# A fused routed feed-forward kernel: block turns on VectorE for the routing, a fifth bank for the first tiles, and a new order of the routing steps

## The chip, the cores and the metric

The kernel runs on one core of one Trainium2 chip. The metric is the device time of one execution in microseconds (us), lower is better. The core has five engines that run their own lists of instructions side by side and meet at semaphores: TensorE (PE, with its weight loads shown as PEld), VectorE (DVE), ScalarE (ACT), GpSimd (POOL) and SyncE (SP), which here only starts transfers. TensorE writes into PSUM, eight banks of 128 partitions by 512 fp32 columns.

## The reference

`x` holds 4 batches of 1024 tokens by 512 features. Each batch has one of 64 condition matrices; eight experts follow, and each token goes to one of them, at most 512 tokens an expert.

```python
h = einsum('bsd,bdh->bsh', x, cond_W[itok]) + cond_b[itok]      # 4096 tokens
probs = softmax(h @ Wr)                      # 8 experts
eidx = argmax(probs);  p_tok = probs[eidx]
rank = number of earlier tokens with the same expert;  keep = rank < 512
xe = h[tokens of expert e, by rank]
ye = (relu(xe @ W1[e]) @ W2[e]) * p_tok      # 512 x 2048, 2048 x 512
out = x + scatter(ye)
```

## The kernel before

**Precision.** The large products are made of three passes over a high and a low part of each operand. ACT copies the high part, VectorE subtracts it to get the low one. A token tile's condition product is 4 blocks of k by 3 passes, twelve matmuls of 512 columns (L1318).

**The stages.** The 32 tiles of 128 tokens (8 chunks of 4 tiles, 2 chunks a batch) go through the condition product first. The first four run together (`first_tiles`, L1302 and L1306) and each later one by `cond_tile`. VectorE's `store_h` adds the bias and writes the tile to `rows` (L864), which frees the bank (`s_accf`). POOL stores whole chunks to memory (L496), SP the last eight tiles one by one (L432). Then the rows of expert 0 are gathered: the early tokens by four indirect transfers from memory (L532), and TensorE turns them into PSUM (L1380); the last four tiles' tokens are added by selection products (L1371). After that an expert loop of Strassen-like W1 products (L1404, L1418) and W2 products (L1506) fills the rest of the time.

**Routing, between the tiles.** The logits are not computed from `h` but from x with a small matrix M = W Wr of the batch, in plain fp32. The steps of a batch are put behind tiles by lists at L50 to L55: the entry for batch b is the tile after which the step runs.
- `M_TURN` (L1208): TensorE multiplies the transposed condition matrix by Wr, in four column groups of 32, for batch 0 with the bias products before it (L1220); ACT copies the result to `m_rows` (L640).
- `M_SUM` (L1228): TensorE turns `m_rows` into PSUM (L1231), and VectorE's `copy_m` writes it to `m32` (L854).
- `ROUTE` (L1233): TensorE multiplies x of the batch's two chunks by M (L1244), 64 products. ACT copies the logits with their bias to `logits_t` (`copy_logits`, L645).
- `CHOOSE`: TensorE turns the logits so that tokens lie on partitions (`by_token`, L1254); VectorE's `choose` takes the maximum and the one-hot rows (L874 to L893); ACT takes the exponentials (L654).
- `PLACE`: TensorE counts ranks (L1262); VectorE's `place` makes the payload and eight selection matrices (L899 to L918).
- `FILL`: TensorE adds the batch to the table of slots (L1273). After the last, the table is turned within the next tile (`turn_table`), and VectorE makes the token lists (`make_tokens`, L967).

`choose_late` (L922) runs on VectorE after the store of tile `PLACE[-1] + 2`. The splits of chunk c stand at tiles `SPLIT_X[c]` (two halves), those of batch b's condition weights at `SPLIT_W[b]` (four blocks), and the first W1 splits at `SPLIT_W1`.

**What sets the order.** Each engine takes its list as written out. For tile n ACT does, in this order, `copy_turned`, `copy_logits`, `exps`, splits of x, splits of W, table copy, W1 split (L679 to L700). VectorE does `store_h`, `choose`, `copy_m`, `place`, `choose_late`, `make_tokens`, late parts, splits of x, of W, of W1 (L1010 to L1037). TensorE does the tile, turn, by-token turn, fill, M turn, rank, route (L1345 to L1358). A low split waits for ACT's high split; `copy_m` must be done before the route; a chunk's load waits for the route that reads the buffer's old chunk.

**Banks.** Three banks serve the tiles in turn, `y_ps` bank 3 the fourth of the first four tiles. So tile 4 waits until tile 0 is stored:

```python
def cond_bank(n):
    return y_ps[:, 3, :] if n == TPC - 1 else cond_ps[n if n < TPC else (n - TPC) % 3]
...
pe.wait_ge(s_accf, n - 3 if n < TPC + 3 else n - 2)
```

**Loads.** SP issues in the order of L354 to L461: condition blocks and x chunks first, then as buffers fall free. Ahead of the first tiles TensorE runs `keep_warm(12)` on zeros (L1336).

Of the kernel before, what the change touches and what calls it, by code (L numbers as in the profile page):

```python
# [17 lines left out]
def moe_kernel(nc, x, x_t, cat, cond_w, cond_wt, cond_b, cond_br, w_r, w_1, w_2, out, h_rows):  # L18
    f32, f32r = mybir.dt.float32, mybir.dt.float32r
    bf16, f16, u32 = mybir.dt.bfloat16, mybir.dt.float16, mybir.dt.uint32  # L20
    ALU = mybir.AluOpType
# [29 lines left out]
    M_SUM = [5, 10, 13, 18]  # L51
    ROUTE = [6, 11, 15, 20]
    CHOOSE = [8, 13, 18, 23]
    PLACE = [10, 15, 20, 25]
    FILL = [13, 18, 23, 27]  # L55

    SPLIT_X = [None, None, (3, 4), (6, 7), (12, 14), (16, 17), (21, 22), (22, 24)]
    SPLIT_W = [None, (4, 4, 5, 5), (11, 11, 12, 13), (16, 17, 18, 19)]
# [4 lines left out]
    SPLIT_W1 = {NT - 9: 0, NT - 8: 3}  # L63
# [23 lines left out]
    with ctx:  # L87
# [39 lines left out]
        m_rows = sb("m_rows", [P, P], f32)  # L127
        ident = sb("ident", [P, P], f32)
# [64 lines left out]
        def cond_bank(n):  # L193
            return y_ps[:, 3, :] if n == TPC - 1 else cond_ps[n if n < TPC else (n - TPC) % 3]
# [3 lines left out]
        turned_ps = y_ps[:, 1, 0:CPB * P].rearrange("p (c n) -> p c n", c=CPB)  # L198
        tok_ps = y_ps[:, 1, 0:CPB * P].rearrange("p (t g) -> p t g", t=TPB)[:, :, 0:E]
# [3 lines left out]
        m_ps = y_ps[:, 3, 0:P]  # L203
        bias_ps = y_ps[:, 3, P:P + BATCH]
        turn_ps = y_ps[:, 3, 2 * P:3 * P]
        logits_ps = tp_ps[:, 0, 0:CPB * P]
        held = [logits_t[:, :, :].rearrange("p c n -> p (c n)"), m32[:, :, :, :].rearrange("p b k g -> p (b k g)")]
# [14 lines left out]
        s_m = sem("m_product_done")  # L222
# [8 lines left out]
        s_lg = sem("logits_done")  # L231
# [110 lines left out]
        def _(sp):  # L342
# [64 lines left out]

            load_next_xt(4)
            load_cond(2)
# [3 lines left out]
            load_next_xt(6)  # L413
            load_next_xt(7)
            load_cond(3)
            sp.wait_ge(s_turn, 3)
            load_cond_wt(3)

# [193 lines left out]
        def _(act):  # L612
# [23 lines left out]
            def copy_turned(b):  # L636
                act.wait_ge(s_turn, b + 1)
                if b >= 1:
                    act.wait_ge(s_m, b)
                nc.scalar.activation(m_rows[:, :], turn_ps, ACTF.Copy).then_inc(s_turnc, 1)  # L640

            def copy_logits(b):
                act.wait_ge(s_mcopy, b + 1)
                act.wait_ge(s_lt, CPB * (b + 1))
                nc.scalar.activation(logits_t[:, :, :].rearrange("p c n -> p (c n)"), logits_ps, ACTF.Identity,  # L645
                                     bias=bias_g[:, b:b + 1]).then_inc(s_ltc, 1)
# [176 lines left out]
        def _(dve):  # L823
# [24 lines left out]
            def copy_m(b):  # L848
                dve.wait_ge(s_m, b + 1)
                if b >= 2:  # L850
                    dve.wait_ge(s_ltc, b - 1)
                if b == 0:
                    nc.vector.tensor_copy(bias_g[:, :], bias_ps)
                nc.vector.tensor_copy(m32[:, b % 2, :, :].rearrange("p k g -> p (k g)"), m_ps).then_inc(s_mcopy, 1)  # L854
# [16 lines left out]
            def choose(b):  # L871

                dve.wait_ge(s_lg, b + 1)
                then(nc.vector.tensor_reduce(top[:, :], tok_ps, AX.X, ALU.max))  # L874
# [3 lines left out]
                nc.vector.tensor_tensor(diff[:, :, :], tok_ps, wide(top[:, :]), ALU.subtract  # L878
# [326 lines left out]
        def _(pe):  # L1205
            PARTS = ((HI, HI), (HI, LO), (LO, HI))

            def m_turn(b):  # L1208
# [13 lines left out]
                for k in range(DK):  # L1222
                    for g in range(NQ):
                        last = nc.tensor.matmul(turn_ps[g * G:(g + 1) * G, :], wr32[:, k, :],  # L1224
                                                stage[:, 0, k, g * P:(g + 1) * P], start=(k == 0), stop=(k == DK - 1))
                last.then_inc(s_turn, 1)

            def m_sum(b):  # L1228

                pe.wait_ge(s_turnc, b + 1)  # L1230
                nc.tensor.transpose(m_ps, m_rows[:, :], ident[:, :]).then_inc(s_m, 1)  # L1231

            def route(b):  # L1233
# [4 lines left out]
                for h in range(CPB):  # L1238
                    c = CPB * b + h
                    if c >= 1:  # L1240
                        pe.wait_ge(s_xin[c % 4], 16 * (c // 4 + (c % 4 > 0)))
                    for k in range(DK):
                        for g in range(NQ):
                            last = nc.tensor.matmul(logits_ps[g * G:(g + 1) * G, h * P:(h + 1) * P], m32[:, b % 2, k, :],  # L1244
                                                    x_in[c % 4][:, k, g * P:(g + 1) * P],
                                                    start=(k == 0), stop=(k == DK - 1))
                    last.then_inc(s_lt, 1)

            def by_token(b):
                pe.wait_ge(s_ltc, b + 1)  # L1250
                if b >= 1:
                    pe.wait_ge(s_oh, b)
                for c in range(CPB):
                    last = nc.tensor.transpose(turned_ps[:, c, :], logits_t[:, c, :], ident[:, :])  # L1254
                last.then_inc(s_lg, 1)
# [84 lines left out]
            keep_warm(KEEP_FIRST)  # L1340
# [4 lines left out]
            for n in range(TPC, NT):  # L1345
# [235 lines left out]
```

## Time and profile before

| | |
|---|---|
| time, median of 3 runs | 800.9 us (799.99 to 800.93) |
| profiled execution, its own time | 800.89 us |
| its span, first to last instruction | 799.0 us |
| PE busy | 791.0 us, 99% |
| DVE busy | 581.1 us, 73% |
| POOL busy | 517.1 us, 65% |
| ACT busy | 351.5 us, 44% |
| mean granted TensorE clock | 0.999 |

The profile is of one execution; its time of 800.89 us is 1.9 us over the span, which runs from the first to the last instruction. Times in the views are microseconds from the span's start. In a view by time a line gives start, length, engine, source line, operation, output and inputs and the count of merged instructions. In brackets stands how long the engine was idle before it, and what ended that. Matmuls overlap, so lengths of single ones add to more than the time they take together; the chain of work gives lengths without the overlap.

### The profile page before, as it was taken

How to read it: one execution, taken by the hardware profiler on the slowest of the kernel's cores; microseconds unless marked ns; L12 is line 12 of the kernel's file. 1: busy time of each engine (PE TensorE's matmuls, PEld its weight loads, DVE VectorE, ACT ScalarE, POOL GpSimd, SP SyncE). 2: the span in 40 equal slices, each digit the busy share in tenths (PEclk: the TensorE clock that was granted, in tenths of full speed). 3: DMA queues.
4: the chain of work that ended last, by engine and by line, in shares of the span. 5: the costliest groups of instructions: out<-in, count | busy, mean ns of one | idle time of the engine just before them, and what ended most of it. 6: DMA issues, size and time to landing. Idle time of an engine off the chain costs nothing.

```text
span 799.0 us, 14228 instructions
## 1 busy us (share of the span) xinstructions
PE 791.0 (99%) x5267; PEld 703.7 (88%) x5267; DVE 581.1 (73%) x760; ACT 351.5 (44%) x537; POOL 517.1 (65%) x392
## 2 busy tenths in 40 slices
PE   8999999999999999999999999999999999999997
PEld 5787889899999999999999999999999999999996
DVE  5677878889767896589658965797578866895532
ACT  4322336446444544445444544454445444554430
POOL 1000138898887688777887688768876888663601
PEclk9999999999999999999999999999999999999999
DMA  8987645542544255534453444435541544255201
GB/s 285 359 297 275 236 131 179 186 142 73 180 170 142 85 181 176 168 105 174 164 163 121 164 164 144 158 110 170 177 145 57 190 154 150 104 184 178 71 1 53
DMA packets 61102, 127.20 MB, mean 159 GB/s; under 512 B 8310, under 2 KB 8310, under 8 KB 60562
## 3 DMA queue, kind: packets, MB, share of 16 engines
q1 hardware_dynamic: 47714, 95.19, 34.3%
q0 software_dynamic: 13216, 31.38, 12.1%
q8 instruction: 17, 0.28, 0.1%
q10 hardware_dynamic: 144, 0.26, 0.1%
q14 instruction: 11, 0.09, 0.0%
HBM read 110.13 MB, written 25.17 MB: 169 GB/s over the span
## 4 chain that ended last, share of the span: by engine, by line
PE 94%; DMA 2%; DVE 2%; issue 1%; SPq 0%; ACT 0%; POOL 0%; POOLq 0%
PE y_ps L1506 44%; PE acc_ps L1404 20%; PE tp_ps L1404 19%; PE acc_ps L1318 5%; PE tp_ps L1318 2%; DMA stage<-x_t 1%; PE tp_ps L1244 1%; DMA early_rows<-h_rows,tok_all 1%; PE acc_ps L1418 1%; PE tp_ps L1418 1%; DVE xt_split L835 1%; PE y_ps L1224 0%; DVE rows L864 0%; PE y_ps L1371 0%; DVE select L918 0%
## 5 line engine op out<-in xcount | busy, mean ns | idle before, releaser
L1506 PE MATMUL y_ps<-w_split,xt_split 128*128 128x512 f32 x1536 | 371.2, 391 | 0.0
L1506 PEld LDWEIGHTS y_ps<-w_split,xt_split 128*128 128x128 f32 x1536 | 280.9, 189 | 53.0
L1404 PE MATMUL acc_ps<-x_split,w_split 128*128 128x256 f32 x1320 | 181.0, 283 | 0.0
L1404 PE MATMUL tp_ps<-x_split,w_split 128*128 128x256 f32 x1284 | 176.5, 283 | 0.0
L1404 PEld LDWEIGHTS acc_ps<-x_split,w_split 128*128 128x128 f32 x1320 | 172.1, 192 | 4.8
L961 DVE TENSOR_TENSOR w_split<-stage,w_split 128x1024 fp32r<-128x1024 f32 x64 | 115.3, 1841 | 81.6 <-ACT w_split L669 81.6
L1404 PEld LDWEIGHTS tp_ps<-x_split,w_split 128*128 128x128 f32 x1284 | 167.7, 192 | 4.9 <-ACT logits_t L728 0.2
L546 POOL DMA_INDIRECT rows<-h_rows,idx_all x112 | 132.3, 1181 | 32.9 <-issue 32.5
L662 ACT ACTIVATE w_split<-stage 128x1024 fp32r<-128x1024 f32 x64 | 53.9, 842 | 92.2 <-PE acc_ps L1404 46.0
L503 POOL TENSOR_TENSOR w_sums<-stage 128x512 f32<-128x512 f32 x31 | 43.0, 1387 | 66.5 <-DVE w_split L950 60.2
L950 DVE TENSOR_TENSOR w_split<-stage,w_split 128x1024 fp32r<-128x1024 f32 x64 | 72.9, 1139 | 15.7 <-ACT w_split L662 15.7
L950 DVE TENSOR_TENSOR w_split<-w_sums,w_split 128x1024 fp32r<-128x1024 f32 x62 | 77.7, 1255 | 5.6 <-ACT w_split L662 5.4
L731 ACT ACTIVATE xt_split<-tp_ps 128x512 fp32r<-128x512 f32 x64 | 38.1, 597 | 79.7 <-PE tp_ps L1404 77.9
L562 POOL DMA_INDIRECT out<-rows,put_all x32 | 37.6, 1175 | 52.5 <-DVE rows L1085 45.0
L731 ACT ACTIVATE xt_split<-acc_ps 128x512 fp32r<-128x512 f32 x64 | 38.0, 598 | 68.9 <-PE acc_ps L1404 67.1
L662 ACT ACTIVATE w_split<-w_sums 128x1024 fp32r<-128x1024 f32 x62 | 65.0, 1049 | 4.2 <-POOL w_sums L506 2.7
L669 ACT ACTIVATE w_split<-stage 128x1024 fp32r<-128x1024 f32 x64 | 64.2, 1060 | 0.0
L1062 DVE SCALAR_TENSOR_TENSOR xt_split<-tp_ps,xt_split 128x512 fp32r<-128x512 f32 x64 | 44.0, 690 | 26.0 <-ACT xt_split L731 25.6
L1062 DVE SCALAR_TENSOR_TENSOR xt_split<-acc_ps,xt_split 128x512 fp32r<-128x512 f32 x64 | 43.9, 688 | 22.4 <-ACT xt_split L731 21.3
L508 POOL TENSOR_TENSOR w_sums<-stage 128x512 f32<-128x512 f32 x31 | 58.7, 1893 | 0.0
L496 POOL DMA_DIRECT2D h_rows<-rows x6 | 4.8, 797 | 82.3 <-DVE rows L864 82.3
L1318 PE MATMUL acc_ps<-w_split,xt_split 128*128 128x512 f32 x228 | 55.1, 394 | 1.2 <-DVE rows L864 1.2
(184 smaller groups left out, 805.5 us busy)
## 6 DMA issues: line engine op xcount, KB each, us to landing
stage<-w SPq DMA_DIRECT2D x64, 1024.0 KB, 7.3
b_rows<-x SPq DMA_DIRECT2D x8, 1024.0 KB, 9.5
h_rows<-rows POOLq DMA_DIRECT2D x6, 1024.0 KB, 9.4
stage<-cond_wt SPq DMA_DIRECT2D x4, 1024.0 KB
x_more<-x_t SPq DMA_DIRECT2D x4, 1024.0 KB, 9.4
stage<-x_t SPq DMA_DIRECT2D x3, 1024.0 KB, 8.1
stage<-cond_w SPq DMA_DIRECT2D x3, 1024.0 KB, 9.5
h_rows<-rows SPq DMA_DIRECT2D x8, 256.0 KB, 2.1
```

The source lines that it names most:

```text
L503: nc.gpsimd.tensor_tensor(w1_sum(0), w1_raw(1, 0, slot), w1_raw(1, 1, slot), ALU.add).then_inc(s_comb, 1)
L508: nc.gpsimd.tensor_tensor(w1_sum(2), w1_raw(0, 0, slot), w1_raw(1, 0, slot), ALU.subtract).then_inc(s_comb, 1)
L546: pool.indirect_dma_start(out=h_quart[:, t * P:(t + 1) * P], out_offset=None, in_=h_parts, in_offset=bass.IndirectOffsetOnAxis(ap=idx_all[ ...
L662: nc.scalar.activation(split_part(w1s, grp, HI), w1_group(grp, slot), ACTF.Copy).then_inc(s_w1hi, 1)
L669: nc.scalar.activation(w2s[:, slot, HI, ks, :], stage[:, 2 + slot, ks, :], ACTF.Copy).then_inc(s_w2hi, 1)
L731: nc.scalar.activation(hts[:, (u % 2) * QF + tile, HI, :], (upper(u) + lower(u))[tile], ACTF.Relu).then_inc(s_hhi, 1)
L950: nc.vector.tensor_tensor(split_part(w1s, grp, LO), w1_group(grp, (u + 1) % 2), split_part(w1s, grp, HI).bitcast(f32), ALU.subtract).then_ ...
L961: nc.vector.tensor_tensor(w2s[:, slot, LO, ks, :], stage[:, 2 + slot, ks, :], w2s[:, slot, HI, ks, :].bitcast(f32), ALU.subtract).then_inc ...
L1062: nc.vector.scalar_tensor_tensor(hts[:, at, LO, :], (upper(u) + lower(u))[tile], 0.0, hts[:, at, HI, :].bitcast(f32), ALU.max, ALU.subtrac ...
L1318: last = nc.tensor.matmul(cond_bank(n), xts[:, c % 4, a, k, t * P:(t + 1) * P], w2s[:, (c // CPB) % 2, w, k, :], start=(k == 0 and (a, w) ...
L1404: last = nc.tensor.matmul(out, w1s[wg][:, w, wb, k, f], xes[xg][:, a, xb, k, :], start=start and k == 0 and (w, a) == (HI, HI), stop=True, ...
L1506: last = nc.tensor.matmul(y_ps[:, s, :], hts[:, (q % 2) * QF + jj, a, s * P:(s + 1) * P], w2s[:, q % 2, w, jj, :], start=(first and jj == ...
```

## The change

1. The M turn and the by-token turn leave TensorE. VectorE turns blocks of 32x32 instead: `copy_m` is a block turn of `m_rows` (128x128), and `choose` begins with a block turn of `logits_t` (128x256) into `by_tok`. For that, the routed products read their columns as four runs of 32 (`group_of`).
2. Tile 4 gets `y_ps` bank 1, free now, and starts when the first half of chunk 1 is split.
3. The lists of steps, splits and loads are new.
4. Two of twelve warming products are replaced by one in fp32 of 256 columns, behind POOL's masks.

```diff
-    M_SUM = [5, 10, 13, 18]
-    ROUTE = [6, 11, 15, 20]
-    CHOOSE = [8, 13, 18, 23]
-    PLACE = [10, 15, 20, 25]
+    M_SUM = [5, 9, 14, 19]
+    ROUTE = [8, 13, 18, 20]
+    CHOOSE = [9, 14, 19, 22]
+    PLACE = [11, 16, 21, 24]
     FILL = [13, 18, 23, 27]
-    SPLIT_X = [None, None, (3, 4), (6, 7), (12, 14), (16, 17), (21, 22), (22, 24)]
-    SPLIT_W = [None, (4, 4, 5, 5), (11, 11, 12, 13), (16, 17, 18, 19)]
+    SPLIT_X = [None, None, (3, 4), (6, 7), (12, 13), (17, 17), (18, 20), (23, 25)]
+    SPLIT_W = [None, (4, 4, 5, 5), (10, 10, 12, 13), (18, 18, 20, 20)]
-    SPLIT_W1 = {NT - 9: 0, NT - 8: 3}
+    SPLIT_W1 = {NT - 9: 0, NT - 7: 3}
...
         def cond_bank(n):
-            return y_ps[:, 3, :] if n == TPC - 1 else cond_ps[n if n < TPC else (n - TPC) % 3]
+            if n in (TPC - 1, TPC):
+                return y_ps[:, 3 if n < TPC else 1, :]
+            return cond_ps[n if n < TPC else (n - TPC - 1) % 3]
...
+            load_cond(2)
             load_next_xt(4)
-            load_cond(2)
             load_next_xt(5)
             sp.wait_ge(s_turn, 2)
             load_cond_wt(2)
-            load_next_xt(6)
-            load_next_xt(7)
             load_cond(3)
             sp.wait_ge(s_turn, 3)
             load_cond_wt(3)
+            load_next_xt(6)
+            load_next_xt(7)
...
             def copy_m(b):
-                dve.wait_ge(s_m, b + 1)
+                dve.wait_ge(s_turnc, b + 1)
...
-                nc.vector.tensor_copy(m32[:, b % 2, :, :].rearrange("p k g -> p (k g)"), m_ps).then_inc(s_mcopy, 1)
+                nc.vector.transpose(m32[:, b % 2, :, :].rearrange("p k g -> p (k g)"), m_rows[:, :]
+                                    ).then_inc(s_mcopy, 1)
...
             def choose(b):
-                dve.wait_ge(s_lg, b + 1)
-                then(nc.vector.tensor_reduce(top[:, :], tok_ps, AX.X, ALU.max))
+                dve.wait_ge(s_ltc, b + 1)
+                nc.vector.transpose(by_tok[:, :, :].rearrange("p t g -> p (t g)"),
+                                    logits_t[:, :, :].rearrange("p c n -> p (c n)")).then_inc(s_lgt, 1)
+                dve.wait_ge(s_lgt, b + 1)
+                then(nc.vector.tensor_reduce(top[:, :], tok_logits, AX.X, ALU.max))
...
+            def group_of(columns, g):
+                return columns.rearrange("p (t a i) -> p a t i", t=NQ, a=NQ)[:, g, :, :]
...
-                                                stage[:, 0, k, g * P:(g + 1) * P], start=(k == 0), stop=(k == DK - 1))
+                                                group_of(stage[:, 0, k, :], g), start=(k == 0), stop=(k == DK - 1))
...
-                                                    x_in[c % 4][:, k, g * P:(g + 1) * P],
+                                                    group_of(x_in[c % 4][:, k, :], g),
...
             def cond_tile(c, t, between=None):
                 n = TPC * c + t
                 if t == 0:
-                    pe.wait_ge(s_xlo, DK + 2 * c)
+                    pe.wait_ge(s_xlo, DK + 2 * c - 1)
                     pe.wait_ge(s_wlo, DK * (c // CPB + 1))
-                pe.wait_ge(s_accf, n - 3 if n < TPC + 3 else n - 2)
+                if n > TPC:
+                    pe.wait_ge(s_accf, n - 4 if n < TPC + 4 else n - 2)
                 for k in range(DK):
+                    if t == 0 and k == 2:
+                        pe.wait_ge(s_xlo, DK + 2 * c)
...
-            keep_warm(KEEP_FIRST)
+            keep_warm(KEEP_FIRST - 2)
+            pe.wait_ge(s_wr0, 2)
+            pe.wait_ge(s_mask, 15)
+            nc.tensor.matmul(acc_ps[:, 1, 0:2 * P], ident[:, :], m32[:, :, :, :].rearrange("p b k g -> p (b k g)"),
+                             start=True, stop=True)
             pe.wait_ge(s_whalf, 1)
...
-                if n in CHOOSE:
-                    by_token(CHOOSE.index(n))
                 if n in FILL:
                     fill_table(FILL.index(n))
-                if n in M_SUM:
-                    m_sum(M_SUM.index(n))
```

## Rows read from the trace of the kernel before

**Rows 1.** The page's first part, busy time and share of each engine.
```profile
PE 791.0 (99%) x5267; PEld 703.7 (88%) x5267; DVE 581.1 (73%) x760; ACT 351.5 (44%) x537; POOL 517.1 (65%) x392
```

**Rows 2.** TensorE in order of time, 0 to 240: start, length, line, work.
```profile
1.36 4.51 PE L1336 MATMUL acc_ps<-zeros,ones 128*128 128x512 bf16 x12 [1.36 <-DVE zeros L993]
6.08 0.69 PE L1302 MATMUL acc_ps<-w_split,xt_split 128*128 128x512 f32 x2 [0.20 <-ACT w_split L633]
...
18.46 2.98 PE L1318 MATMUL acc_ps<-w_split,xt_split 128*128 128x512 f32 x12 [1.15 <-DVE rows L864]
21.38 0.44 PE L1220 MATMUL y_ps<-b_col,wr 128*32 128x4 f32 x32
...
22.66 3.02 PE L1318 MATMUL acc_ps<-w_split,xt_split 128*128 128x512 f32 x12
...
114.96 0.75 PE L1380 MATMUL y_ps<-ident,early_rows 128*128 128x128 f32 x4 [0.33 <-DMA early_rows<-h_rows,tok_all]
```

**Rows 3.** VectorE in order of time, 0 to 60 us.
```profile
19.43 0.68 DVE L864 TENSOR_TENSOR rows<-y_ps,b_rows 128x512 f32<-128x512 f32 x1
...
32.01 1.23 DVE L835 TENSOR_TENSOR xt_split<-x_more,xt_split 128x1024 fp32r<-128x1024 f32 x1 [2.74 <-ACT xt_split L618]
```

**Rows 4.** VectorE in order of time, 60 to 135 us.
```profile
72.90 0.23 DVE L874 TENSOR_REDUCE top<-y_ps 128x8 f32<-128x64 f32 x1 [0.69 <-PE y_ps L1254]
...
75.06 0.29 DVE L854 COPY m<-y_ps 128x128 f32<-128x128 f32 x1
...
96.15 0.69 DVE L950 TENSOR_TENSOR w_split<-stage,w_split 128x512 fp32r<-128x512 f32 x1 [0.75 <-ACT w_split L662]
...
97.36 0.21 DVE L899 TENSOR_REDUCE total<-expo 128x8 f32<-128x64 f32 x1
...
101.63 0.68 DVE L864 TENSOR_TENSOR rows<-acc_ps,b_rows 128x512 f32<-128x512 f32 x1
102.23 0.68 DVE L864 TENSOR_TENSOR rows<-tp_ps,b_rows 128x512 f32<-128x512 f32 x1
...
104.14 0.29 DVE L967 COPY table<-y_ps 128x128 f32<-128x128 f32 x1
```

**Rows 5.** The chain that ended last, 0 to 270 us: start, length, what.
```profile
28.54 1.89 PE tp_ps L1244 x64
...
36.09 1.01 PE y_ps L1224 x32
37.10 0.37 PE y_ps L1254 x2
...
47.80 2.94 PE tp_ps L1318 x12
50.75 2.72 PE acc_ps L1318 x12
...
54.85 0.56 PE y_ps L1273 x32
...
79.22 1.88 PE tp_ps L1244 x64
```

**Rows 6.** Weight loads of lines 1380 and 1231: ns minimum, median, maximum.
```profile
L1380 PEld LDWEIGHTS y_ps<-ident,early_rows x16: 194/212/220, 113.3 to 116.5; 128*128 128x128 f32 x16
...
L1231 PEld LDWEIGHTS y_ps<-ident,m_rows x4: 138/141/142, 25.3 to 73.3; 128*128 128x128 f32 x4
```

**Rows 7.** GpSimd in order of time, 0 to 20 us.
```profile
3.75 0.61 POOL L490 CAST spread_w<-ident 128x512 f16<-128x512 f32 x1
```

**Rows 8.** ScalarE in order of time, 0 to 120 us.
```profile
30.56 0.47 ACT L645 ACTIVATE logits_t<-tp_ps,bias_g 128x256 f32<-128x256 f32 x1 [4.48 <-PE tp_ps L1244]
```

**Rows 9.** Line 1068, the block turn of the expert loop.
```profile
L1068 DVE STREAM_TRANSPOSE turned<-rows x28: 1067/1092/1122, 173.2 to 680.5; 128x512 f32<-128x512 f32 x28
```

**Rows 10.** Line 375, loads of x chunks, from issue to landing.
```profile
DMA to landing us min/median/max: 5.6/9.0/13.8
```

**Rows 11.** Line 532, gathers of early rows, from issue to landing.
```profile
DMA to landing us min/median/max: 3.8/4.6/6.0
```

More of the change, by code:

```diff
@@ L127, in moe_kernel @@
         m_rows = sb("m_rows", [P, P], f32)
+        by_tok = sb("by_tok", [P, TPB, G], f32)
         ident = sb("ident", [P, P], f32)
@@ L193, in cond_bank @@
         def cond_bank(n):
-            return y_ps[:, 3, :] if n == TPC - 1 else cond_ps[n if n < TPC else (n - TPC) % 3]
+            if n in (TPC - 1, TPC):
+                return y_ps[:, 3 if n < TPC else 1, :]
+            return cond_ps[n if n < TPC else (n - TPC - 1) % 3]
         slots_ps = y_ps[:, 0, 0:P]
         table_ps = y_ps[:, 3, 0:SB * E * Q].rearrange("p (s e q) -> p s e q", s=SB, e=E)
-        turned_ps = y_ps[:, 1, 0:CPB * P].rearrange("p (c n) -> p c n", c=CPB)
-        tok_ps = y_ps[:, 1, 0:CPB * P].rearrange("p (t g) -> p t g", t=TPB)[:, :, 0:E]
         rank_ps = y_ps[:, 2, 0:TPB * E]
@@ L202, in moe_kernel @@
         idx_ps = tp_ps[:, 0, 2 * P:2 * P + NQ * E * SB].rearrange("p (q e s) -> p q e s", q=NQ, e=E)
-        m_ps = y_ps[:, 3, 0:P]
         bias_ps = y_ps[:, 3, P:P + BATCH]
@@ L206, in moe_kernel @@
         logits_ps = tp_ps[:, 0, 0:CPB * P]
+        tok_logits = by_tok[:, :, 0:E]
         held = [logits_t[:, :, :].rearrange("p c n -> p (c n)"), m32[:, :, :, :].rearrange("p b k g -> p (b k g)")]
@@ L221, in moe_kernel @@
         s_turnc = sem("m_turned_copied")
-        s_m = sem("m_product_done")
         s_mcopy = sem("m_copied")
@@ L230, in moe_kernel @@
         s_ltc = sem("logits_t_copied")
-        s_lg = sem("logits_done")
+        s_lgt = sem("logits_turned")
         s_diff = sem("diff_done")
@@ L638, in copy_turned @@
                 if b >= 1:
-                    act.wait_ge(s_m, b)
+                    act.wait_ge(s_mcopy, b)
                 nc.scalar.activation(m_rows[:, :], turn_ps, ACTF.Copy).then_inc(s_turnc, 1)
@@ L644, in copy_logits @@
                 act.wait_ge(s_lt, CPB * (b + 1))
+                if b >= 1:
+                    act.wait_ge(s_lgt, b)
                 nc.scalar.activation(logits_t[:, :, :].rearrange("p c n -> p (c n)"), logits_ps, ACTF.Identity,
@@ L877, in choose @@
                 chained[0] += 1
-                nc.vector.tensor_tensor(diff[:, :, :], tok_ps, wide(top[:, :]), ALU.subtract
+                nc.vector.tensor_tensor(diff[:, :, :], tok_logits, wide(top[:, :]), ALU.subtract
                                         ).then_inc(s_diff, 1)
@@ L1224, in m_turn @@
                         last = nc.tensor.matmul(turn_ps[g * G:(g + 1) * G, :], wr32[:, k, :],
-                                                stage[:, 0, k, g * P:(g + 1) * P], start=(k == 0), stop=(k == DK - 1))
+                                                group_of(stage[:, 0, k, :], g), start=(k == 0), stop=(k == DK - 1))
                 last.then_inc(s_turn, 1)
-            def m_sum(b):
-                pe.wait_ge(s_turnc, b + 1)
-                nc.tensor.transpose(m_ps, m_rows[:, :], ident[:, :]).then_inc(s_m, 1)
             def route(b):
@@ L1244, in route @@
                             last = nc.tensor.matmul(logits_ps[g * G:(g + 1) * G, h * P:(h + 1) * P], m32[:, b % 2, k, :],
-                                                    x_in[c % 4][:, k, g * P:(g + 1) * P],
+                                                    group_of(x_in[c % 4][:, k, :], g),
                                                     start=(k == 0), stop=(k == DK - 1))
                     last.then_inc(s_lt, 1)
[L1249 to L1255, printed above, removed]
             def rank_of(b):
```

## The prediction

> **What bounds the kernel now.** I read the page first: TensorE is busy for 791.0 of the 799.0 us [rows 1]. So the time is TensorE's list of work plus its waits. The view of waits puts those within the first 260 us, so I read TensorE's order of time there, where the whole change lies. It starts on the first four tiles when ACT's split of the first weights comes (6.08), stands still for 1.15 us before tile 4, because the bank is still to be emptied by VectorE, and does bias and first turn from 21.38 to 22.66. After that no wait is worth a number until the gathered early rows, where it goes on at 114.96 after 0.33 us [rows 2]. Behind that nothing stops it, so a microsecond won or lost by then is one of the total.
>
> The second thing to see is what stands close behind TensorE: VectorE's order of time in the same stage. It takes every result out of PSUM, splits all operands and does the choosing and placing, one after another; its fourth store ends at 20.11 [rows 3]. The store of tile 27 (102.23, 0.68 long, done at 102.91 [rows 4]) sends the last early rows to memory, from where they are gathered, and TensorE goes on with them 12.05 us later. It was already waiting then: VectorE's lateness at tile 27 decides when TensorE may go on.
>
> **TensorE's own sum.** *First bank.* Tile 4 gets a bank that nobody holds, and needs only the first half of chunk 1. It starts at 18.46 - 1.15 = 17.31 and ends at about 20.2. The first turn wants the fourth store, visible at about 20.25, and takes its 1.28: tile 5 begins at 21.5 in place of 22.66, 1.15 sooner, and the turn waits up to 0.2 where tile 4 waited before.
> *Visits.* The two products that turn the logits are 0.37, four times; a turn of M is at least its weight load of 0.14, four times [rows 5, 6]. A tile that follows small products takes 2.94 for 2.72 [rows 5], so fewer visits save some 0.2 each. The new order from 21.5: tiles 5 to 8, 2.94 + 3 x 2.72 = 11.1; a turn 1.01 and a route 1.88 (35.5); tiles 9 to 13 with a rank in between, 14.0 (49.5); turn, fill 0.56, route, 3.45 (52.9); tiles 14 to 18, 14.0 (66.9); 3.45 again: **the third route ends at 70.35**; tiles 19 and 20, 5.66: TensorE reaches the fourth route at 76.0, where before it did at 79.2 [rows 5] with the same work left but the last turn of logits (0.37). The saving so far is 3.2; with that turn and the wait for the early rows (0.33) it would be **3.9 us if nothing else stopped it**.
> *Block columns.* The routed products read four runs of 32 columns instead of one of 128. The bias products already read elements 16 bytes apart, 32 of them in 0.44 us [rows 2]; I take no cost. The far bound: a weight load of strided fp32 takes 212 ns where a plain one takes 141 [rows 6]; half as much again on all turns and routes would be 5.8 us. No column less is read, so there is no gain.
> *Warming.* The twelve bf16 products run from 1.36 to 5.87 [rows 2]; ten end near 5.4. The fp32 product of 256 columns I put between 0.45, two products at the tiles' pace of 2.72/12 = 0.227, and twice that; it ends by 6.3 at the latest, and the first tile waits for ACT until 6.08 anyway. It adds a wait for POOL's last mask, done at 4.36 [rows 7]: nothing. Two tenths lost here are covered by the fourth store at 20.25.
>
> **VectorE's and ACT's sum, where the change bites.** ACT copies the logits when a route is done and only then takes the splits listed at that tile. Before, a route with a split behind it stood at tile 6: ACT's copy began at 30.56 [rows 8], VectorE's split followed at 32.01 after 2.74 us of standing still [rows 3]. That route ended at 30.43 [rows 5], so VectorE's next split comes 1.58 behind a route. In the new lists splits of chunk 6 and of the fourth condition weights stand at tiles 18 and 20, both tiles of a route, and the M turn for the last route stands at 19, behind choosing. Unit costs, as starts of neighbours [rows 3, 4]: store 0.60; split of a half chunk 1.22 less the same overlap of 0.08, 1.14; condition split 0.60; choosing 75.06 - 72.90 = 2.16; placing 101.63 - 97.36 = 4.27; late choosing 104.14 - 102.83 = 1.31, 102.83 being 102.23 + 0.60.
> *Block turns.* VectorE has a block turn of 128x512 at 1.09 us [rows 9]. Half of it, 0.55, and a quarter, 0.28, each with 0.04 of handshake; bounds: the rate of a store (0.34 and 0.17) below, the whole row and half of it above (1.09 and 0.55). I take the share, it being the same operation. The Trainium skill (Vector Engine (DVE) Microarchitecture Reference, 3.8 The reshape front-end and per-opcode configuration) says that the turn sustains one element per cycle and lane. The row here, 2.1 ns an element, is twice as slow as that at the 0.96 GHz which its first page (Trainium Kernel Development and Optimization, NeuronCore Architecture) gives; three turns at that rate would be 0.7 us shorter, an estimate that makes the forecast 802.8.
> *The chain.* Third route ends 70.35; +1.58 = 71.93. VectorE: split 1.14, two condition splits 1.2, store 19 0.6, turn 0.59, choosing 2.16, M turn 0.32: 77.94. TensorE stood at the fourth route from 76.0: **a wait of 1.9 us in place of the one removed.** Behind it on TensorE are all later tiles; ACT and VectorE wait for the route. Route to 79.85; +1.58 = 81.4. Then VectorE without a pause: split and two condition splits 2.34, store 21 0.6, placing 4.27, store 22 0.6, turn 0.59, choosing 2.16, store 23 0.6, split 1.14, W1 split of the same shape 1.14, store 24 0.6, placing 4.27, store 25 0.6, split 1.14, the wait for ACT's last W1 split 0.75 (as at 96.15 in [rows 4]), that split 0.6, store 26 0.6, late choosing 1.31, store 27 0.68. Sum 24.0: **tile 27 is stored at about 105.5, before it was at 102.91**. Late choosing stands ahead of store 27 now, since the last placing moved from 25 to 24 and it follows two tiles on; that alone is 1.31 of it.
> So the early rows come 2.6 later. TensorE, done with tile 31 near 112.2, waits among the gathers until 117.55, where before it went on at 114.96. Fill 2 waits some 0.4 on placing, beside the chain. Next behind: W1 sums on POOL wait for the late parts, which follow tile 31's store and so end no later than before.
> *Queues.* SP has load 2 of the condition weights before chunk 4, and chunks 6 and 7 behind the fourth condition weights and their transpose. Those wait for VectorE's last condition split at tile 13, near 56.4, so four megabytes and bias rows go out from there. Loads of this line land 5.6 to 13.8 after issue [rows 10]; chunk 6, third in line, is wanted by ACT at 70.85, and the transposed weights by TensorE at 66.9. I count nothing, at most 2 us.
>
> **Sum.** 3.9 us of TensorE's work and waits go, and 6.5 of waiting come (1.9 at the fourth route, 0.4 at fill 2, 4.2 at the early rows): +2.6 on the profiled execution's 800.89, which is the median of the runs too (800.9). **Forecast 803.5 us.** What a measurement of this kernel can tell is about 0.2%, 1.6 us.
>
> **Rivals.**
> *A, VectorE's chain as summed*: 803.5; by the bounds of the turns (-0.55, +1.35) 802.9 to 804.9. For it: the same pattern at tile 6 in the trace. Chance 0.56.
> *B, the same and the clock falls.* In the last microseconds before 117.55 TensorE would only do short transposes between waits. At the start of the trace, after standing idle, twelve products of 512 columns took 4.51 us [rows 2] where the tiles' pace gives 2.72, so it ran part of them at 1.2 GHz and lost 1.8. The same here: 805.3. Against it: the twelve products right after the 1.15 us wait took 2.98, full clock [rows 2]. The Trainium skill (TensorE: Matmul & The Clock Gate, Part 4: PE-mode transpose) says that transposes do not count as busy in the same way; no row here shows it. Chance 0.17.
> *C, the early rows land sooner.* The slowest of the four gathers took 6.0 from issue to landing, the median 4.6 [rows 11]. At the median the wait is 1.4 shorter: 802.1. Chance 0.12.
> *D, faster.* TensorE's saving carries through: 800.9 - 3.9 = **797.0**. It needs VectorE to store tile 27 by about 99, so it turns on the 1.58 behind the third and fourth routes and on the backlog. The program's order on both engines speaks against it; for it, that VectorE stood still for 2.74 at tile 6 at no cost. Chance 0.15.
> That the visits are fewer and the 1.15 goes is plain from the program, so I give no chance to the change not doing what it says.
>
> **How the numbers follow.** Slower is A and B, 0.73; within is C, 0.12; faster is D, 0.15. The range of 800.6 to 806.2 takes in A, B and C, and leaves out D and a little above (strided columns that cost, a chunk that lands late).
>
> **What would show it.** Right: the wait before tile 4 gone, one of at most 0.4 before the first turn; a wait near 2 us at the fourth route, released by the M turn; store 27 some five microseconds behind tile 27's end; waits of some 4 us at the early rows, none after; a block turn of 128x256 near 0.55. Wrong: tile 27 stored before 102, or no wait at the fourth route; routes of over 2 us (strides); products at more than 0.227 apart after 117 (B).

## The result and the profile after

| | before | after |
|---|---|---|
| time, median | 800.9 us (799.99 to 801.19, 6 runs) | **804.5 us** (803.47 to 806.19, 6 runs) |
| profiled execution, its own time | 800.89 us | 803.47 us |
| its span | 799.0 us | 801.8 us |
| ratio after / before | | 1.0048 [1.0038, 1.0057] |

Slower by half a per cent, with the whole interval above the 0.2% that a measurement here can tell. The forecast was 803.5 us. The profiled execution is 2.58 us slower than that of before, where +2.6 was summed; the median is 1.0 us above the profiled execution, which happens to be the lowest of the six.

The first and second part of the page of the kernel after, cut to the lines used (busy time and share of each engine, then the granted clock in 40 slices):

```profile
span 801.8 us, 14206 instructions
...
PE 789.5 (98%) x5255; PEld 702.7 (88%) x5255; DVE 575.2 (72%) x764; ACT 352.2 (44%) x537; POOL 512.4 (64%) x392
...
PEclk9999999999999999999999999999999999999999
```

TensorE does 12 instructions and 1.5 us less than in [rows 1], yet the span is 2.8 us longer: what it gained it stands still for, and more. TensorE's waits in the first 260 us of the kernel after say where (total, times, longest):

```profile
PE y_ps L1379 <- DMA early_rows<-h_rows,tok_all: 2.9, 2, 1.5
PE tp_ps L1248 <- DVE m L856: 2.5, 1, 2.5
PE acc_ps L1335 <- DVE zeros L999: 1.4, 1, 1.4
PE acc_ps L1298 <- ACT w_split L633: 0.4, 1, 0.4
PE y_ps L1269 <- DVE select L924: 0.4, 1, 0.4
```

The 1.15 us before tile 4 [rows 2] are gone. In their place are 2.5 us at the fourth route (L1248), released by VectorE's turn of M (the block turn of `m_rows` that the list `M_SUM` places, called the M turn below), and 2.9 for the gathered early rows where there were 0.33. TensorE in order of time, kernel after:

```profile
5.59 0.98 PE L1342 MATMUL acc_ps<-m,ident 128*128 128x256 f32 x2
...
18.01 2.98 PE L1317 MATMUL y_ps<-w_split,xt_split 128*128 128x512 f32 x12
20.92 0.44 PE L1229 MATMUL y_ps<-b_col,wr 128*32 128x4 f32 x32
21.20 1.08 PE L1233 MATMUL y_ps<-stage,wr 128*32 128x128 f32 x32
22.20 5.74 PE L1317 MATMUL acc_ps<-w_split,xt_split 128*128 128x512 f32 x24
...
68.66 1.93 PE L1248 MATMUL tp_ps<-stage,m 128*32 128x128 f32 x64
70.52 3.01 PE L1317 MATMUL tp_ps<-w_split,xt_split 128*128 128x512 f32 x12
...
78.79 1.96 PE L1248 MATMUL tp_ps<-x_more,m 128*32 128x128 f32 x64 [2.54 <-DVE m L856]
...
117.66 0.75 PE L1379 MATMUL y_ps<-ident,early_rows 128*128 128x128 f32 x4 [1.49 <-DMA early_rows<-h_rows,tok_all]
```

TensorE is at the fourth route at 78.79 - 2.54 = 76.25, nearly three microseconds before it was there in [rows 5], and stops. It goes on with the third block of early rows at 117.66, 2.70 later than in [rows 2], and nothing stops it after that. VectorE in the same stage, kernel after:

```profile
72.85 1.23 DVE L837 TENSOR_TENSOR xt_split<-x_more,xt_split 128x1024 fp32r<-128x1024 f32 x1 [2.57 <-ACT xt_split L618]
...
75.80 0.43 DVE L877 STREAM_TRANSPOSE by_tok<-logits_t 128x256 f32<-128x256 f32 x1
...
78.43 0.31 DVE L856 STREAM_TRANSPOSE m<-m_rows 128x128 f32<-128x128 f32 x1
...
82.36 1.22 DVE L837 TENSOR_TENSOR xt_split<-x_more,xt_split 128x1024 fp32r<-128x1024 f32 x1 [3.05 <-ACT xt_split L618]
...
104.97 0.74 DVE L938 TENSOR_SCALAR late_sel<-iota_c,late_rel 128x128 bf16<-128x128 f16 x4
105.63 0.68 DVE L867 TENSOR_TENSOR rows<-acc_ps,b_rows 128x512 f32<-128x512 f32 x1
```

VectorE stands for 2.57 us behind ACT's split of chunk 6, reaches the M turn at 78.43, stands for 3.05 behind the fourth route, and is then without a pause, but for the 0.75 us behind ACT's W1 split that the forecast had too, until the store of tile 27 is done at 106.31; late choosing is right ahead of that store. The chain of waits of the kernel after shows the transfers in it, and SP's issue of the fourth condition weights ahead of the chunk (start, length):

```profile
56.92 0.38 SPq L405
...
58.43 13.31 DMA x_more<-x_t
71.76 1.07 ACT xt_split L618
...
106.34 2.02 DMA h_rows<-rows
...
112.18 5.44 DMA early_rows<-h_rows,tok_all
```

ACT could have split chunk 6 at 71.19, when its copy of the logits was done, and began at 71.76. The chunk was asked for at 58.43 only, behind the fourth condition weights, for which SP stood until 56.92. How empty the transfers were before that is in the table of stretches, 48 to 57 us, where the last two columns are their share and GB/s. The kernel before:

```profile
48.00:57.00 9.00, 9.00 (x98) 7.04 (x98) 7.00 (x17) 4.79 (x9) 0.75 (x1) 1.00 0.97 333
```

The kernel after, same stretch:

```profile
48.00:57.00 9.00, 9.00 (x154) 7.57 (x153) 6.56 (x13) 2.22 (x4) 0.00 (x0) 1.00 0.20 74
```

### The profile page after: what moved, and what is told of

Read it like the earlier page. It is cut to its first block, busy times and chain, and to the rows that moved or that the text cites. A ratio compares the mean times of both kernels' runs of the same rounds, so it can differ in the third digit from the quotient of the medians.

```text
span 801.8 us, 14206 instructions
## 1 busy us (share of the span) xinstructions
PE 789.5 (98%) x5255; PEld 702.7 (88%) x5255; DVE 575.2 (72%) x764; ACT 352.2 (44%) x537; POOL 512.4 (64%) x392
## 4 chain that ended last, share of the span: by engine, by line
PE 90%; DMA 3%; DVE 3%; issue 2%; ACT 1%; SPq 0%; POOL 0%; POOLq 0%; ACTq 0%
PE y_ps L1505 44%; PE acc_ps L1403 20%; PE tp_ps L1403 19%; PE acc_ps L1317 2%; DMA x_more<-x_t 2%; PE tp_ps L1317 1%; PE acc_ps L1417 1%; PE tp_ps L1417 1%; PE tp_ps L1248 1%; DMA early_rows<-h_rows,tok_all 1%; DMA stage<-cond_w 1%; ACT xt_split L618 1%; DVE xt_split L837 0%; DVE rows L867 0%; DVE w_split L847 0%
## 5 line engine op out<-in xcount | busy, mean ns | idle before, releaser
L967 DVE TENSOR_TENSOR w_split<-stage,w_split 128x1024 fp32r<-128x1024 f32 x64 | 114.1, 1821 | 84.0 <-ACT w_split L671 84.0
L503 POOL TENSOR_TENSOR w_sums<-stage 128x512 f32<-128x512 f32 x31 | 43.2, 1395 | 69.4 <-DVE w_split L956 66.5
L956 DVE TENSOR_TENSOR w_split<-stage,w_split 128x1024 fp32r<-128x1024 f32 x64 | 71.1, 1112 | 16.8 <-ACT w_split L664 16.7
L956 DVE TENSOR_TENSOR w_split<-w_sums,w_split 128x1024 fp32r<-128x1024 f32 x62 | 75.6, 1220 | 6.1 <-ACT w_split L664 6.0
L508 POOL TENSOR_TENSOR w_sums<-stage 128x512 f32<-128x512 f32 x31 | 60.2, 1941 | 0.0
L506 POOL TENSOR_TENSOR w_sums<-w_sums,stage 128x512 f32<-128x512 f32 x31 | 52.6, 1696 | 2.4
```

Of the source, the lines that this page charges most:

```text
L503: nc.gpsimd.tensor_tensor(w1_sum(0), w1_raw(1, 0, slot), w1_raw(1, 1, slot), ALU.add).then_inc(s_comb, 1)
L506: nc.gpsimd.tensor_tensor(w1_sum(1), w1_sum(0), w1_raw(0, 0, slot), ALU.subtract).then_inc(s_comb, 1)
L508: nc.gpsimd.tensor_tensor(w1_sum(2), w1_raw(0, 0, slot), w1_raw(1, 0, slot), ALU.subtract).then_inc(s_comb, 1)
L956: nc.vector.tensor_tensor(split_part(w1s, grp, LO), w1_group(grp, (u + 1) % 2), split_part(w1s, grp, HI).bitcast(f32), ALU.subtract).then_ ...
L967: nc.vector.tensor_tensor(w2s[:, slot, LO, ks, :], stage[:, 2 + slot, ks, :], w2s[:, slot, HI, ks, :].bitcast(f32), ALU.subtract).then_inc ...
```

## The experiments

The theory: all of the loss is in the new lists, which put splits, choosing and the M turn ahead of the fourth route on VectorE and late choosing ahead of store 27; turns, bank and warming cost nothing. The rival causes are strided operands, the block turns, the warming and the clock.

### The lists put back

```diff
-    ROUTE = [8, 13, 18, 20]
+    ROUTE = [6, 11, 15, 20]
...
-            load_cond(2)
             load_next_xt(4)
+            load_cond(2)
...
```

All seven lists of the kernel after, and the order of its loads, as they were before.

> All lists of steps, splits and loads are put back to those of before; block turns, the fifth bank and the warming product stay. Theory (the new order puts VectorE's and ACT's work behind the third and fourth routes, and with it the store of tile 27): no wait at the fourth route, tile 27 stored near 101.5, the early rows sooner than in the kernel before by 1.3, so about 799.5 in a profiled execution, 4 us under the changed kernel; TensorE waits about 1.1 for the selection at tile 27. Rival 1 (the new operations themselves cost: strided columns, block turns on VectorE): it stays at 803 or more. Rival 2 (the time is lost to a lower clock after waits): as the theory, since the waits go too.

Measured: 798.87 us (798.5 to 799.56), ratio to before 0.9973 [0.9963, 0.9984], faster than both kernels. No wait stands at the fourth route. Its waits:

```profile
PE acc_ps L1298 <- ACT w_split L633: 1.3, 2, 1.0
PE y_ps L1269 <- DVE select L924: 0.9, 1, 0.9
PE y_ps L1379 <- DMA early_rows<-h_rows,tok_all: 0.3, 1, 0.3
```

So the rest of the change wins about 1.9 us, and the lists on top of it lose 5.6 (804.5 less 798.87).

### The lists alone, on the kernel before

```diff
-    ROUTE = [6, 11, 15, 20]
+    ROUTE = [8, 13, 18, 20]
...
```

> The kernel before with nothing but the new lists of steps, splits and loads; the turns stay on TensorE, four banks, twelve warming products. Theory: slower than before by about as much as the changed kernel or more, since TensorE's turns are still there: tile 27 stored near 107, 804.9 (+4); a wait of about 1 us at the fourth route. Rival 1 (the new operations cost): at the time of before, 800.9 within 1 us.

Measured: 804.65 us (803.59 to 806.51), 1.0056 [1.0037, 1.0074]. The waits of this kernel:

```profile
PE y_ps L1380 <- DMA early_rows<-h_rows,tok_all: 2.8, 2, 2.0
...
PE tp_ps L1244 <- DVE m L854: 1.1, 1, 1.1
PE acc_ps L1318 <- DVE rows L864: 0.6, 1, 0.6
```

The same two waits without any other part of the change. The lists alone make the whole loss, whatever turns the logits; with them in, what the rest of the change wins cannot be told (804.65 and 804.5).

### The last M turn a tile earlier

```diff
-    M_SUM = [5, 9, 14, 19]
+    M_SUM = [5, 9, 14, 18]
```

> The changed kernel with one entry changed: the M turn of the last batch stands at tile 18 in place of 19, so before the choosing. Theory: the wait of 2.5 us at the fourth route goes whole, but VectorE is then behind by its own work, so only about 1.8 of it reaches tile 27's store: 104.5, and 801.7 in a profiled execution. Rival 1: the wait is not what ends late, 803.5 as the changed kernel. If the whole wait counted: 801.0.

Measured: 801.12 us (800.47 to 803.03), 1.0008 [0.9999, 1.0018]; profiled 800.92. TensorE of this kernel at the fourth route, and at the third block of early rows:

```profile
76.27 1.95 PE L1248 MATMUL tp_ps<-x_more,m 128*32 128x128 f32 x64
...
115.12 0.75 PE L1379 MATMUL y_ps<-ident,early_rows 128*128 128x128 f32 x4 [1.62 <-DMA early_rows<-h_rows,tok_all]
```

The wait is gone, and the early rows come 117.66 - 115.12 = 2.54 us sooner: exactly the wait. I had expected a part of it only. VectorE's second chain hangs on the fourth route through ACT's copy, so all that the route waits reaches store 27. One number in one list is worth 2.5 of the 2.6 us between the profiled executions of before and after; by the medians it is 3.4 of the 5.6 that the lists cost on top of the rest.

### Late choosing behind store 27

```diff
-                if n == PLACE[-1] + 2:
+                if n == PLACE[-1] + 3:
```

> The changed kernel with the late choosing one tile later, so behind the store of tile 27 and not ahead of it. Theory: the store of tile 27 comes 1.3 sooner (105.0), the early rows too: 802.2 in a profiled execution. Rival: the late choosing, still ahead of the token list, holds the gathers as before, since they wait for the token list too: 803.5. By the theory the list (107.0) is ready before the store has landed (107.1), so nearly all of the 1.3 shows.

Measured: 801.13 us (800.06 to 803.19), 1.0009 [0.9999, 1.0018]. The profiled one, 802.01 us, shows something else too. TensorE of this kernel in order of time, VectorE's stores of tiles 26 and 27, and the table of stretches around the route (third column from the right: granted clock):

```profile
78.33 3.34 PE L1248 MATMUL tp_ps<-x_more,m 128*32 128x128 f32 x64 [2.54 <-DVE m L856]
```

```profile
104.67 1.28 DVE L867 TENSOR_TENSOR rows<-acc_ps,b_rows 128x512 f32<-128x512 f32 x2
```

```profile
76.00:78.50 2.50, 0.17 (x4) 0.17 (x8) 2.19 (x11) 0.26 (x1) 0.47 (x1) 0.86 1.05 393
78.50:81.00 2.50, 2.50 (x52) 2.30 (x52) 0.35 (x1) 0.00 (x0) 0.00 (x0) 0.50 0.92 369
81.00:82.00 1.00, 1.00 (x22) 0.74 (x15) 0.00 (x0) 0.20 (x1) 0.00 (x0) 0.88 0.10 41
```

In the 2.54 us wait the granted clock fell to half (1.2 GHz), and the route behind it took 81.60 - 78.33 = 3.27 us for the 1.89 of the kernel after: 1.4 us that the wait costs beyond its own length. TensorE then came to the early rows too late to wait for them. The five fastest executions of this kernel, with a mean clock of 0.998 to 0.999, are at 800.06 to 800.82. That is 2.7 to 3.4 below the one execution of the kernel after at a mean clock of 1.000 (803.47), where 1.3 was summed: the 802.01 near the expected 802.2 is luck, since it holds the 1.4 that the clock cost. What was summed is there: from the start of the fourth route to the end of store 27 it is 27.62 us here (78.33 to 105.95) and 27.52 in the kernel after (78.79 to 106.31), with the route 1.4 longer, so 1.3 less but for the clock. The rest was not summed; a part of it is that the four gathers landed 3.6 to 4.7 us after issue, in the kernel after 3.8 to 5.4, and why they did is open.

### Chunks 6 and 7 ahead of the fourth condition weights

```diff
             load_cond_wt(2)
+            load_next_xt(6)
+            load_next_xt(7)
             load_cond(3)
...
-            load_next_xt(6)
-            load_next_xt(7)
```

> The changed kernel with chunks 6 and 7 loaded ahead of the fourth condition weights and their transpose again, as before. In the changed kernel ACT waited 0.57 us for chunk 6 at the third route. Theory: that wait goes and all behind it on VectorE comes 0.6 sooner: tile 27 stored near 105.7, 802.9 where the clock stays up, and the wait at the fourth route 1.9 as forecast. Rival: the condition weights now come late in their place and hold the last M turn or the splits at tile 18: 803.5 or more.

Measured: 805.5 us (803.66 to 807.98), 1.0066 [1.0045, 1.0086]: the rival. The interval overlaps that of the kernel after, so a gain of 0.6 is not there and a loss is not shown. Its waits:

```profile
PE y_ps L1379 <- DMA early_rows<-h_rows,tok_all: 2.6, 2, 1.4
PE tp_ps L1248 <- DVE m L856: 1.8, 1, 1.8
PE y_ps L1233 <- DMA stage<-cond_wt: 1.6, 1, 1.6
```

The chunk is no longer late; the transposed condition weights for the last `M_TURN`, behind tile 18, are, by 1.6 us. In this stage two loads want the same time; exchanging them only names another one.

### The three together

> The changed kernel with the three single edits together: last M turn at tile 18, late choosing behind the store of tile 27, chunks 6 and 7 loaded first. Theory: they lie on one chain one after another and add up, about 1.8 + 1.3 + 0.6 = 3.7 us: tile 27 stored near 102.6, 799.9 to 800.6, about the kernel before; no wait at the fourth route, so the clock has no cause to fall there. Rival (each removes a wait that the next one puts back): 802.

Measured: 800.19 us (799.27 to 801.04), 0.9988 [0.9979, 0.9998]. The new lists with the M turn, late choosing and loads mended are back at the time before, still 1.3 us above the old lists with the rest of the change. That is inside what was expected, but partly by luck, since the parts do not add up: alone, the M turn and the late choosing each took 3.4 us off the median of the kernel after and the chunks put 1.0 on to it, and the three together take 4.3 off. In the trace the transposed condition weights are late again (1.1 us), and the third block of early rows comes at 115.36, no sooner than with the M turn alone (115.12).

### Bank, turns and warming apart

Each on the kernel before, with its lists. The bank:

> The kernel before with the fifth bank for tile 4 and the wait on half a chunk alone. Theory: the 1.15 us before tile 4 goes, and up to 0.2 of it comes back before the first turn; TensorE is 1.0 earlier until the early rows, where VectorE, which stood idle for 0.9 before the store of tile 22, passes about 0.9 on: 800.0. Rival: VectorE's chain to tile 27 is the bound already and nothing moves: 800.9.

Measured: 800.29 us (799.49 to 801.06), 0.9992 [0.9983, 1.0001]. Tile 4 does not wait, and the early rows come at 114.05 where it was 114.96. Too small to tell from nothing in the medians.

The block turns, with the strided operands:

> The kernel before with the block turns alone (the columns of the operands in block order, the M sums and the by-token turns on VectorE); old bank, old lists, old order of loads, old warming. The theory: the end of this stage is set by VectorE's chain to store 27 and the gather behind it, so what TensorE saves (three by-token turns of 0.37 us and the M turns ahead of the early rows, some 1.5 us) comes through only as far as VectorE's stores follow TensorE around tile 22, less 0.43 us for the block turn itself: 800.2 to 800.8 us (0 to 0.6 sooner than the kernel before), with TensorE's wait for the early rows up from 0.33 us to about 1.3. The rival, that the saved TensorE time counts whole: 799.3 us and a wait for the early rows as before.

Measured: 799.69 us (799.0 to 800.01), 0.9981 [0.9971, 0.9990], between the two. The wait for the early rows, which was to grow, is gone; a selection is waited for in its place:

```profile
PE y_ps L1267 <- DVE select L922: 0.9, 1, 0.9
PE acc_ps L1312 <- DVE rows L865: 0.2, 1, 0.2
```

Both together, with the old warming:

> The kernel after with all lists and the order of the loads as before (the version that measured 798.9), and with the old warming of 12 bf16 products. The theory, that the warming decides nothing: 798.9 us, within 0.3, the granted clock 1.00 from the first tile on in both. The rival, that the fp32 product delays the first tiles: 798.6 or less. The other rival, that it holds the clock: 799.4 or more, with a granted clock under 1 in the first 20 us.

Measured: 798.98 us (798.26 to 799.75), 0.9979 [0.9969, 0.9990]. That is the 798.87 with the fp32 product, within the spread: the warming decides nothing, and the granted clock is 1.00 in both from the start.

### A version below both

The old lists with the rest of the change leave 0.9 us of waiting at the fourth fill, behind VectorE's list. One W1 split and its wait for ACT can stand behind store 27:

```diff
-    SPLIT_W1 = {NT - 9: 0, NT - 8: 3}
+    SPLIT_W1 = {NT - 9: 0, NT - 4: 3}
```

> The kernel after with the lists and loads of before, except that the second split of the first W1 (0.63 us on ScalarE, 0.69 us on VectorE and 0.75 us of its waiting) is put behind tile 28 instead of tile 24, so that it no longer stands ahead of the selection of the fourth batch and of store 27. The theory: the selection ends some 1.3 us sooner, the wait of the fourth fill (0.9 us) and that for the early rows (0.3 us) go, and the late split has slack behind it: 797.7 us. The rival, that the split is late for the first products of W1 or for the next load into its buffer: 798.9 us or more, with a wait for that split or that load in TensorE's waits.

Measured: **797.95 us** (797.61 to 798.88), 0.9964 [0.9952, 0.9977]. All of TensorE's waits that its first 260 us have left:

```profile
PE acc_ps L1335 <- DVE zeros L999: 1.4, 1, 1.4
PE tp_ps L1248 <- DVE m L856: 0.3, 1, 0.3
```

### New lists, written anew

Routes behind tiles 8, 13, 18 and 21, splits taken off the tiles of the routes, late choosing four tiles behind the last placing, chunks first.

```diff
-    ROUTE = [8, 13, 18, 20]
-    PLACE = [11, 16, 21, 24]
+    ROUTE = [8, 13, 18, 21]
+    PLACE = [11, 16, 21, 23]
...
```

> The changed kernel with lists in which no split that VectorE needs soon stands behind a route on ACT: M turn of batch 1 at 10, last route at 21, last placing at 23, late choosing at 27, splits of x (12, 12), (13, 15), (16, 18), (22, 24), of condition weights (10, 11, 12, 13), (16, 17, 17, 19), first W1 splits at 22 and 26, chunks 6 and 7 loaded first. Theory: TensorE is the bound again and its own saving shows: tile 27 stored within 1 us of its end (near 99.6), no wait at routes, at most 0.3 at the early rows, 797.6. Rival 1 (the new operations cost): not under 800. If loads come late for the earlier splits: 798.5 to 800.

Measured: 800.75 us (800.21 to 801.68), 0.9997 [0.9988, 1.0006]: a miss by 3 us. VectorE of this kernel, and then GpSimd:

```profile
92.47 2.50 DVE L907 CAST payload<-prob 128x8 f16<-128x8 f32 x1
```

```profile
92.36 0.75 POOL L496 DMA_DIRECT2D h_rows<-rows  x1 [15.10 <-DVE rows L867]
93.11 1.83 POOL L568 MEMSET early_rows<- 128x2048 f32 x1
```

A cast of eight elements a partition took 2.50 us and ended with GpSimd's zeroing of a buffer (94.97 and 94.94). Its like takes 0.18. To test that, GpSimd's zeroing was held until the last selection:

```diff
             pool.wait_ge(s_acc, NT - 8)
+            pool.wait_ge(s_sel, BATCH)
             nc.gpsimd.memset(early_rows[:, :, :], 0.0).then_inc(s_zero, 1)
```

> The version with the mended lists (800.75 us), with one wait added: GpSimd's zeroing of the early rows' buffer (1.83 us) starts after the fourth batch's selection. In that version VectorE's cast of 128x8 elements at 92.47 us, whose like takes 0.18 us, took 2.50 us and ended with that zeroing. The theory, that the cast stood still for the zeroing: the cast is 0.18 us again, the fourth selection ends 2.3 us sooner, TensorE's 1.8 us of waiting for a store at 97.6 us goes, and the time is 798.7 to 799.3 us. The rival, that the cast was long for another reason (the copy of the rows that GpSimd issued at 92.36 us): still long, 800.75 us.

Measured: 798.72 us (797.47 to 798.88), 0.9966 [0.9955, 0.9977], 2.0 below. VectorE of this version, the cast and one split that now lies beside the zeroing, then GpSimd:

```profile
92.21 0.18 DVE L908 CAST payload<-prob 128x8 f16<-128x8 f32 x1
...
96.64 1.22 DVE L838 TENSOR_TENSOR xt_split<-x_more,xt_split 128x1024 fp32r<-128x1024 f32 x1
```

```profile
92.10 0.75 POOL L496 DMA_DIRECT2D h_rows<-rows  x1 [15.10 <-DVE rows L868]
96.25 1.81 POOL L569 MEMSET early_rows<- 128x2048 f32 x1 [3.39 <-DVE select L925]
```

The issue of the copy lies beside the cast here too, and the cast is short: it was the zeroing. What is left of the miss (798.72 for the 797.6 expected) is likely TensorE's longest wait in this trace, 1.8 us for the transposed condition weights at the last `M_TURN`, as in the version with the chunks first; no run takes it away. So lists with fewer, larger visits are not worse in themselves: this version is level with the old lists (798.87) and within 0.8 us of the best version.

## Why the prediction was right, point by point

**The mechanism is the one summed in case A**: VectorE's two chains, the wait at the fourth route, store 27 late, the early rows late. The lists alone give all of it, and moving the M turn by one tile takes 2.5 of the 2.6 us away.

**Its terms.**

| step | summed | measured |
|---|---|---|
| tile 4 starts | 17.31 | 18.01 |
| tile 5 starts | 21.5 | 22.20 |
| third route ends | 70.35 | 70.52 |
| TensorE at the fourth route | 76.0 | 76.25 |
| split behind the third route | 71.93 | 72.85 |
| M turn done | 77.94 | 78.74 |
| wait at the fourth route | 1.9 | 2.54 |
| wait at fill 2 | 0.4 | 0.35 |
| second chain, split to store 27 done | 24.0 | 23.95 |
| store 27 done | 105.5 | 106.31 |
| from there to TensorE going on | 12.05 | 11.35 |
| waits among the early rows | 4.2 | 2.9 |
| TensorE goes on | 117.55 | 117.66 |

The waits that came are 5.8 us (2.54, 0.35 and 2.86) where 6.5 was summed. With 2.58 between the profiled executions, some 3.2 went where 3.9 was summed. Both sides were 0.7 too large and cancel, so the +2.6 is met that closely by luck; the sign and the places are not.

*First bank and warming.* The wait is gone, but tile 5 is 0.46 sooner, not 1.15. The ten bf16 products ended at 5.79, not 5.4, the fp32 one after them at 6.57, not by 6.3, and the third product of the first tiles started at 6.87, before at 6.61. Then a wait of 0.36 for the split of the condition weights came at 9.69. The fourth store did not hide these, since TensorE's own work runs through to tile 5. Neither is a property of the change: the ten products took 3.81 us with the lists put back, and the second wait is 1.0 there and absent in the version with the W1 split moved, which starts alike.

*Visits.* Right to 0.3 us at the fourth route, though tile 5 began 0.7 late: a turn (`M_TURN`) and a route behind each other are 34.21 - 33.31 = 0.90 and 36.07 - 34.21 = 1.86, not 1.01 and 1.88.

*Block columns.* No cost: 273 ns a routed product, for 274 before.

*Block turns.* 0.43 and 0.31 us, for the 0.55 and 0.28 taken; inside the bounds. The share of the 1.09 us row [rows 9] was the wrong way to size them: the two shapes, 434 and 311 ns for 256 and 128 elements, differ by 0.96 ns an element and have 188 ns fixed, where that row has 2.1 ns an element. It reads every fourth element of its source (L1065), the two new turns read theirs in a row; that this makes the difference was not tested. The pace that the Trainium skill states (Vector Engine (DVE) Microarchitecture Reference, 3.8 The reshape front-end and per-opcode configuration), one element per cycle and lane, at the 0.96 GHz of the forecast an estimate of 1.04 ns, is close to the 0.96 ns measured; with the fixed part the turns still cost more than by the pace alone.

*Loads.* Counted as nothing, at most 2 us: this is the term that was mis-sized. The loads of that line took 7.9 to 15.8 us to land, where [rows 10] had 5.6 to 13.8. Chunk 6 was 0.57 us late, that moved the M turn and with it the wait (2.54 for 1.9) and store 27. What I left out is that the transfers lie idle (share 0.20) while SP stands at the fourth condition weights.

*Gathers.* The last that counted took 5.44 us, where the forecast kept 6.03 from the trace of before (the slowest of [rows 11]), and gave 0.6 back. TensorE ended tile 31 at 113.4, not 112.2, so it waited less there for the same end. So TensorE goes on within 0.1 us of the forecast by two errors of opposite sign, store 27 0.8 late and the way from there 0.7 short: luck too.

**The rivals.** *C* is part of the truth by that 0.6 us. *D* fell at the lists, not at the rest: turns and bank do give 1.9 us, and with a W1 split moved 2.7 us (800.66 to 797.95), where TensorE's own sum had 3.9. *B* put the fall of the clock at the early rows, and took its price from the slow products at the start, as work at 1.2 GHz. The granted clock does not bear that out: in the tables of stretches it is 1.00 over the warming products in the kernel before, and over the early rows in the kernel after (third column from the right).

```profile
0.00:7.00 7.00, 5.43 (x16) 2.33 (x17) 2.16 (x9) 2.96 (x4) 3.54 (x21) 1.00 0.51 165
```

```profile
102.00:120.00 18.00, 15.13 (x103) 12.49 (x92) 12.44 (x28) 6.32 (x11) 7.06 (x6) 1.00 0.52 156
```

Why the warming products are slow stays open. One profiled run, with the late choosing moved, shows the clock fall at the fourth route instead, for +1.4 us. The version with the M turn a tile earlier has no wait there, yet its ten executions run from five at 800.47 to 800.95 us with a mean clock of 1.000 to one at 803.03 with 0.995, so it falls in other places too. The six runs of the kernel after line up in much the same way: 803.47 us at 1.000, 803.99 to 805.23 at 0.996 to 0.997, 806.19 at 0.994. With the chunks first it is not so: 803.66 at 0.998, 804.83 at 1.000. A fall of the clock would fit the 1.0 us between median and profiled execution; that it makes it, and where the clock fell in those runs, is not shown.

## What to carry to other kernels

When work is moved on an engine that is off the critical path, write its list out to the next step that the critical engine waits for: here one M turn listed behind choosing was worth 2.5 us, because TensorE, which waits, also feeds VectorE's list again. Fewer, larger visits save the small handovers, but bring splits, choosing and loads to the same place; look at the transfers' idle stretches before a load is put behind a wait. Try the parts of a change apart: three that win can hide under one that loses.

## What the runs showed of the hardware

- In one profiled execution TensorE's granted clock fell during a wait of 2.54 us, to half (1.2 GHz): it was 0.86 in the stretch of 76.0 to 78.5 us, 0.50 in that of 78.5 to 81.0, 0.88 in that of 81 to 82. In the kernel after, the same wait of 2.54 us passed at 1.00.
- GpSimd's zeroing of 128x2048 held a VectorE cast for 2.3 us longer than its like. The Trainium skill (SBUF — State Buffer, SBUF: two separate sides) says that VectorE and GpSimd share a pair of ports as an exclusive lock, for a VectorE instruction in a two-port mode, or one with two inputs in SBUF against a GpSimd one that reads SBUF: the one that starts first has it until it ends. The trace agrees that the cast stood until the zeroing ended, and that a split of two fp32 inputs beside the zeroing, which reads nothing, kept its 1.22 us. It does not show which started first (the cast's record begins 0.64 us ahead of the zeroing's), nor the mode of the cast.
- The warming products, alike in every version with as many, took 4.47 to 5.28 us for twelve and 3.66 to 4.43 for ten, from one profiled execution to the next, with a granted clock of 1.00 over the first 6 us in each.
- Outside the span (time less span) every execution of a version with the block turns spends 1.64 to 1.75 us, and every one without them 1.81 to 1.96. So some 0.2 us of the turns' gain lie outside the trace; no run here shows why.
